# A transformer layer's attention keys: block-diagonal rows placed by DMA from DRAM images instead of by GpSimd products

## The reference

```python
x = _layernorm(x + _L0_attn_ref(x, Wq, bq, Wk, bk, Wv, bv))          # self-attention with interleaved rotary q, k
x = _layernorm(x + _L0_xattn_ref(x, ctx_1024, ctx_1024, mask, ...))  # 64 context rows, additive mask, dense after it
x = _layernorm(x + _L0_ffn_ref(x, W1, b1, W2, b2))                   # 128 -> 512 relu -> 128
# attention: scores = einsum('bhqd,bhkd->bhqk', q, k) / sqrt(8); softmax; einsum('bhqk,bhkd->bhqd', probs, v)
```

## Time and profile before

| | |
|---|---|
| median of 3 runs | 338.19 us (336.9 to 339.77) |
| profiled execution, span | 337.1 us |
| PE busy | 255.9 us (76%) |
| DVE busy | 225.2 us (67%) |
| ACT busy | 158.3 us (47%) |
| POOL busy | 151.3 us (45%) |
| DMA queue of SP | 20.86 MB, 22.7% of 16 engines |

### The profile page before, as it was taken

The page is one execution under the profiler, slowest core; times in us unless marked ns, Lnnn a source line. Parts: engine busy times, 40 slices in busy tenths (PEclk is TensorE's granted clock), DMA queues, the critical chain, the costliest instruction groups (busy, mean ns, idle before and its releaser), DMA issues.

```text
span 337.1 us, 5516 instructions
## 1 busy us (share of the span) xinstructions
PE 255.9 (76%) x1800; PEld 185.0 (55%) x1800; DVE 225.2 (67%) x471; ACT 158.3 (47%) x297; POOL 151.3 (45%) x159
## 2 busy tenths in 40 slices
PE   3146788779789889788978897888798786766752
PEld 1134355456566577566756665577476655544532
DVE  6534464867796877887788978877888464331322
ACT  1003347345666567455755764566357635305211
POOL 0027347539639733964296439633741321410010
PEclk9999989979999979997999999979799997957859
DMA  7232023115024211521152115111420120120000
GB/s 249 79 70 70 16 45 105 35 52 159 21 66 135 62 35 34 148 62 39 27 148 62 36 35 150 43 33 35 118 50 8 45 88 8 47 58 2 17 0 16
DMA packets 25413, 21.11 MB, mean 63 GB/s; under 512 B 6577, under 2 KB 22065, under 8 KB 25265
## 3 DMA queue, kind: packets, MB, share of 16 engines
q1 hardware_dynamic: 25392, 20.86, 22.7%
HBM read 8.79 MB, written 3.67 MB: 37 GB/s over the span
## 4 chain that ended last, share of the span: by engine, by line
PE 47%; DVE 34%; issue 9%; ACT 6%; DMA 1%; SPq 1%; POOL 0%; DVEq 0%; POOLq 0%; ACTq 0%
DVE neg_max L822 8%; PE scores_qk L389 7%; PE scores_kq L401 6%; DVE x L849 6%; PE pv_acc L422 5%; PE tail_ps L571 5%; PE tail_ps L606 4%; PE scores_qk L443 3%; DVE neg_maxx L894 3%; PE scores_qk L446 2%; DVE var_eps L844 2%; ACT probs L688 2%; PE scores_kq L465 1%; DVE max_parts L829 1%; DVE y L849 1%
## 5 line engine op out<-in xcount | busy, mean ns | idle before, releaser
L822 DVE TENSOR_REDUCE neg_max<-scores_qk 128x4 f32<-128x1024 f32 x64 | 78.1, 1221 | 33.5 <-PE scores_qk L389 32.8
L688 ACT ACTIVATE probs<-scores_kq 128x1024 f32<-128x1024 f32 x64 | 65.5, 1024 | 45.2 <-PE scores_kq L401 44.6
L293 POOL TENSOR_TENSOR k_diag<-slots,second_sb 128x1024 fp32r<-128x1024 f32 x31 | 58.7, 1892 | 29.8 <-DMA slots<-qk_parts 29.7
L389 PE MATMUL scores_qk<-k_diag,slots 96*128 96x512 f32 x128 | 47.5, 454 | 21.4 <-DVE neg_max L822 11.2
L401 PE MATMUL scores_kq<-slots,k_diag 128*128 128x256 f32 x256 | 49.8, 319 | 3.1 <-ACT probs L688 3.0
L401 PEld LDWEIGHTS scores_kq<-slots,k_diag 128*128 128x128 f32 x256 | 38.2, 205 | 11.2 <-issue 7.4
L1015 POOL TENSOR_TENSOR rstd<-var_eps,minus_half 128x2 f32<-128x2 f32 x24 | 16.8, 699 | 61.0 <-DVE var_eps L844 60.5
L422 PE MATMUL pv_acc<-probs,v_ones 128*32 128x256 f32 x512 | 36.7, 407 | 0.0
L389 PEld LDWEIGHTS scores_qk<-k_diag,slots 96*128 96x128 f32 x128 | 21.2, 206 | 26.6 <-issue 15.7
L1058 POOL TENSOR_TENSOR qx_parts<-qx,qx_parts 128x256 fp32r<-128x256 f32 x8 | 5.9, 733 | 46.7 <-DVE qx_parts L984 46.7
L849 DVE TENSOR_SCALAR x<-sum,mean_var,rstd 128x128 f32<-128x128 f32 x32 | 23.1, 764 | 0.8 <-POOL rstd L1015 0.8
(11 more groups left out here) (111 smaller groups left out, 489.1 us busy)
## 6 DMA issues: line engine op xcount, KB each, us to landing
slots<-qk_parts SPq DMA_DIRECT2D x96, 64.0 KB, 2.0
qx_slots<-qx_scratch SPq DMA_DIRECT2D x24, 128.0 KB, 2.7
qk_swapped<-qk SPq DMA_DIRECT2D x16, 128.0 KB, 2.3
qx_scratch<-qx_parts SPq DMA_DIRECT2D x8, 256.0 KB, 2.0
later_sb<-later SPq DMA_DIRECT2D x1, 1347.0 KB, 8.2
x_in<-x SPq DMA_DIRECT2D x8, 128.0 KB, 2.4
x_res<-x SPq DMA_DIRECT2D x8, 128.0 KB, 2.3
out<-y SPq DMA_DIRECT2D x8, 128.0 KB, 1.9
```

Of the source, the lines that this page charges most:

```text
L293: ops.tensor_tensor(k_diag[:, g, :, :].bitcast(F32R), slots[:, g, 1:2, :].to_broadcast([P, HQ, S]), row_head.to_broadcast([P, HQ, S]), ALU ...
L389: mm = pe.matmul(scores_qk[:, h * S:(h + 2) * S], sp_r[0:NROWS, g, 0, t * P:(t + 1) * P], kd_r[0:NROWS, g, h:h + 2, :], start=True, stop=True)
L688: nc.scalar.activation(probs[:, g % 2, 2 * half:2 * half + 2, :, :], scores_kq[:], ACT.Exp).then_inc(exp_done[g][half], 1)
L822: nc.vector.tensor_reduce(neg_max[:, g, t, :], scores_qk[:].rearrange("p (h k) -> p h k", k=S), AX.X, ALU.max, negate=True).then_inc(max_d ...
```

## The change

k's block-diagonal rows are no longer made by POOL. For self-attention, SP writes `qk_parts` to a DRAM image `z_self` in three DMAs (q high twice, k high twice, and both low parts), waits until they have landed, and loads from it `q_rows` (one DMA) and `k_diag` (four, one for each head position h, to every fourth partition). The zeros between are written once at the start: DVE clears `k_diag[:, 0]`, `kx_diag` and rows of `q_rows`, POOL clears `k_diag[:, 1]`. The columns for rows 96 to 103 are then copied once by ACT from `head_of_row`. `q_rows` and `k_diag` are double: element n uses part (n - 1) mod 2. To let one DMA reach the rows of a head, heads and dimensions are renumbered in the columns of the weights and biases: row p holds head 4 (p mod 4) + (p / 4 mod 4), and the rotary partner is 64 rows away, so that the swap goes by halves. Cross-attention gets images `z_kx` and `z_qx` in the same way. The hardware loop is written out, and counts are constants.

The core of the diff:

```diff
+        z_self = [nc.dram_tensor(f"z_self{b}", [8, P, S], F32, kind="Internal").ap() for b in range(2)]
+        z_qx = nc.dram_tensor("z_qx", [3, P, S], F32, kind="Internal").ap()
+        z_kx = nc.dram_tensor("z_kx", [3, P, SC], F32, kind="Internal").ap()
...
-        slots = sb("slots", [P, QUADS, 2, S])
-        k_diag = sb("k_diag", [P, QUADS, HQ, S])
+        q_rows = sb("q_rows", [P, 2, QUADS, S])
+        k_diag = sb("k_diag", [P, 2, HQ, QUADS, S])
...
-        def diagonal(eng, ops, g, loaded, used):
-
-            eng.wait_ge(slots_in[g], loaded)
-            if used:
-                eng.wait_ge(exp_ready[g][1], used)
-            ops.tensor_tensor(k_diag[:, g, :, :].bitcast(F32R), slots[:, g, 1:2, :].to_broadcast([P, HQ, S]),
-                              row_head.to_broadcast([P, HQ, S]), ALU.mult).then_inc(diag_done[g], 1)
...
+            def row_images(r):
+                z = z_self[r.n % 2].rearrange("(j s) p c -> p j s c", j=2)
+                if r.s > 1:
+                    sp.wait_ge(rows_in[(r.n - 1) % 2], 80 * ((r.n - 1) // 2))
+                sp.wait_ge(qk_hi_done, r.n)
+                for j in range(2):
+                    sp.dma_start(z[:, j, 0:2, :], qk_parts[:, 2 * j:2 * j + 1, :].to_broadcast([P, 2, S])
+                                 ).then_inc(z_hi_out, 16)
+                sp.wait_ge(qk_lo_done, r.n)
+                sp.dma_start(z[:, 0, 2:4, :], qk_parts[:, 1:4:2, :]).then_inc(z_lo_out, 16)
+
+            def row_loads(r):
+                b = (r.n - 1) % 2
+                z = z_self[r.n % 2]
+                q_image = z[0:3].rearrange("s (r g) c -> (s r) g c", g=QUADS)
+                k_image = z[3:6].rearrange("s (r h g) c -> (s r) h g c", h=HQ, g=QUADS)
+                sp.wait_ge(z_hi_out, 32 * r.n)
+                sp.wait_ge(z_lo_out, 16 * r.n)
+                if r.starts_prep:
+                    sp.wait_ge(diag_zeroed, 2)
+                if r.m:
+                    sp.wait_ge(exp_ready[3][1], r.m)
+                sp.dma_start(q_rows[0:NROWS, b, :, :], q_image).then_inc(rows_in[b], 16)
+                for h in range(HQ):
+                    sp.dma_start(k_diag[h:NROWS:HQ, b, h, :, :], k_image[:, h, :, :]).then_inc(rows_in[b], 16)
...
                 if r.prep:
-                    slot_loads(0, r.n, r.s)
-                    slot_loads(1, r.n, r.s)
+                    row_images(r)
+                    row_loads(r)
...
             def max_scores(g, t, done, free, free_count):
-
-                pe.wait_ge(diag_done[g], done)
+                b = (done - 1) % 2
+                pe.wait_ge(rows_in[b], 80 * ((done + 1) // 2))
+                if done == 1:
+                    pe.wait_ge(diag_ready, 3)
...
             act.wait_ge(first_in, 16)
-            iterations(act, "act", "w n n_32 s m t u", body)
+            act.wait_ge(diag_zeroed, 2)
+            for b in range(2):
+                for h in range(HQ):
+                    ins = nc.scalar.copy(k_diag[NROWS:NROWS + MROWS, b, h, :, :].bitcast(F32R), row_head(h, QUADS, S))
+                ins.then_inc(diag_ready, 1)
+            for h in range(HQ):
+                ins = nc.scalar.copy(kx_diag[NROWS:NROWS + MROWS, :, h, :].bitcast(F32R), row_head(h, QUADS, SC))
+            ins.then_inc(diag_ready, 1)
+            iterations(body)
...
-            nc.vector.memset(slots[NROWS:P, :, 0, :], 0.0)
-            nc.vector.memset(slots[NROWS:P, :, 1, :], 1.0)
+            nc.vector.memset(k_diag[:, 0, :, :, :], 0.0)
+            nc.vector.memset(kx_diag[:], 0.0)
+            nc.vector.memset(q_rows[NROWS:P, :, :, :], 0.0).then_inc(diag_zeroed, 1)
             nc.vector.memset(qx_slots[NROWS:P, :, :], 0.0)
-            nc.vector.memset(kx_slots[NROWS:P, :, :], 1.0)
...
+            nc.gpsimd.memset(k_diag[:, 1, :, :, :], 0.0).then_inc(diag_zeroed, 1)
```

More of the change, by code:

```diff
@@ L263, in rope_cosine, with iterations @@
+        def iterations(body):
+            for e in range(-2, B + 3):
+                body(Counts(e))
         def rope_cosine(eng, ops, r):
@@ L354, in body @@
+                    z = z_qx.rearrange("s p c -> p s c")
+                    sp.dma_start(z[:, 0:2, :], qx_parts[:, 0:1, :].to_broadcast([P, 2, S])).then_inc(qx_out, 16)
+                    sp.dma_start(z[:, 2, :], qx_parts[:, 1, :]).then_inc(qx_out, 16)
                 if r.mid:
[L355 removed]
+                    sp.wait_ge(kx_out, 32 * r.m)
                     if r.t:
                         sp.wait_ge(expx_ready[1], r.t)
[L358 to L360 removed]
+                    k_image = z_kx.rearrange("s (r h g) c -> (s r) h g c", h=HQ, g=QUADS)
@@ L693, in maxT @@
                 for t in range(QT):
-                    ins = nc.scalar.copy(slots[NROWS:NROWS + MROWS, g, 0, t * P:(t + 1) * P].bitcast(F32R),
+                    ins = nc.scalar.copy(q_rows[NROWS:NROWS + MROWS, (done - 1) % 2, g, t * P:(t + 1) * P].bitcast(F32R),
                                          prep_ps[t * P // QT:t * P // QT + MROWS, 0:P])
@@ L1090, in shape_constants @@
     sin = ((sign * np.sin(angle.astype(np.float64)))[:, None, :] * scale).reshape(P, 2 * S)
-    head = np.where(row < NROWS, (row % QROWS) // HD, np.where(row < NROWS + MROWS, row % HQ, -1))
+    head = np.where(row < NROWS + MROWS, row % HQ, -1)
     return {
@@ L1108 @@
     every_row = lambda v: np.broadcast_to(v[None, :], (P, v.shape[0]))
+    row = np.arange(P)
+    head_of = 4 * (row % 4) + row // 4 % 4
+    rotary = HD * head_of + 2 * (row // 16 % 4) + row // 64
+    plain = HD * head_of + row // 16
     maskT = a["mask_1x1xSxS2_fk1"][0, 0].T
```

179 lines of the change are left out of this document (56 added, 123 removed).

## The result

Four runs of the changed kernel have a median of 349.93 us (349.13 to 353.5), four of the kernel before on the same chip 338.5: a ratio of 1.037, 95% interval 1.030 to 1.044. It is slower by 11 us where 6.5 us less were forecast, and outside the range. The profiled span is 347.3 us against 337.1.

A forecast was written before the change was run, and what follows sets the result against it. TensorE sets the floor and waits for VectorE, which POOL's products hold up. Span 337.1 + 12.3 + 2.2 + 0.5 - 21.5 = 330.6; with 1.1 from span to median, 331.7 us; range 322 to 344.

The forecast's parts named there:

- The mechanism of the gain: VectorE instructions with SBUF operands stand still while POOL computes its products: 24.6 us of VectorE time, y's normalise more.
- the unrolled loop: Writing out the hardware loop, only three of eleven iterations: nothing, between -1 and +2 us.
- the three rivals: Stalls move house, rows land too late, or start costs little and the stalls all go (323.6 us, chance 0.15).
- The stalls move house: Rival: POOL's rope products start sooner and block VectorE instead; half the gains return, 342.4 us, chance 0.15.
- The rows land too late: Rival: the five row loads land after the first scores want them; 345.7 us at 2 us each, chance 0.12.
- Moved on SP's queue: SP's transfers reordered behind the images; kx_diag and qx_slots needed only in the next iteration: nothing.
- The two hops: DMA to a DRAM image and back, qk_low to first scores: 7.0 us, so +2.2 us at the start.
- slow end: Upper estimate of the two DMA hops, from later_sb's transfer rate: 8.3 us after qk_low.
- The cover: Steady iterations: 9.45 us from qk_low's end to the scores needing new rows, hides the hops and does not shrink.
- +0.5: Iteration 0: only 6.6 us from qk_low to the scores, rows up to 1.7 us late, taken as +0.5 us.
- The start's first term: Clearing and head-row casts before ScalarE's first xT copy, which starts at 18.2 in place of 5.86: +12.3 us.
- The gains: POOL's products removed: shorter VectorE stalls and TensorE waits, and no clock fall at L571, 21.5 us in sum.

The follow-up runs named there:

- the unread products: The changed kernel with POOL products of the old sizes put back, written to a buffer nobody reads or waits for: 368.08 us.
- the late casts: The changed kernel, with ScalarE copying the first element's xT and qk before it waits for the clearing and writes the twelve head-row casts: 335.6 us.

## Why the prediction was wrong

*The mechanism of the gain* held. VectorE's stall beside POOL's products is shown by the unread products. The gain is in the last three iterations before the drain (101.1 us before, 89.9 after), where L571 no longer takes 3.56 us. TensorE's waits for att1 before the drain fell by 6.5 us where 6.0 were counted, those at L600, 4.1 in all, are gone from the list, and the unrolled loop is worth nothing. None of the three rivals is what happened. "The stalls move house" is excluded by x's 339 ns and var_eps' 169 ns; what stayed is y's normalise at 528 ns, for example 1.59 us for a pair at 154.96 with POOL's qk_cos running from 155.19, and it had 746 before. "The rows land too late" happened in part, 6.5 us in five waits, 4.9 of them in iterations 1 and 2. For the largest part of the miss, the order on SP's queue, I had no rival.

*The step that failed* is "Moved on SP's queue": "kx_diag and qx_slots are needed only in the next iteration ... Nothing." By the program's counting that is true, but the next iteration begins a few us later: L416 at 160.11 uses what was issued at 156.19. I counted issues ("four and one in place of three and three") and gave them no length. With an issue time of 0.81 us for each kx load, the four put 3.2 us between the qx images and qx_slots. With these loads first the span is 8.2 us shorter. 5 us of it are waits, and the late casts give the same 5; the others come with a clock whose cause is open. I had looked at the steady iteration alone, where this is covered, and not at the drain, where qx_slots has no cover: there the kernel before already showed 1.16 us of waiting.

*The two hops* were mis-sized. "I take 7.0" between 5.9 and 8.3: measured 8.5 us from the end of qk_low to the scores at the start, beyond the slow end, and 9.3 in iteration 1 (qk_low ends at 80.9, L364 starts at 90.21). The issue term, 4 x 0.45 = 1.8, was 3.1; the image landed in 2.75 instead of 2.0. The strided loads' issue had no row in the trace of before, and I bounded it by the issue of transfers of another shape.

*The cover* was mis-sized the other way. "It does not shrink" was wrong: L571, now L544, lies between and went from 3.56 to 1.89 us by the very gain that I had counted. The kernel before could have told: one iteration on, with L571 at 1.89 us, the distance is 8.6 us (from 189.66 to 198.26), and 0.62 of these are TensorE's wait at L600 that I had counted as a gain too. After the change TensorE reaches the next scores after some 8 us, while the rows take up to 8.7, and it waits 0.2 to 1.2 us (from 170.33, the end of qk_low, to the scores at 178.95 with a wait of 0.61; from 200.49 to 209.23 with 0.72). In iteration 1 the kernel before had only 7.6 us (from 63.38 to 70.94), less than my slow end of 8.3; I had looked at iteration 0 and a steady one. There the rows took 9.3 us and TensorE waited 3.8. So "+0.5" for late rows was 6.5 us.

*The start's first term* was right: +12.3 forecast, +12.8 measured. Two small errors partly cancel in it: the clearing was over at 8.5 instead of 7.4, and the casts took 8.9 us instead of 9.5 (0.955 each for the wide ones, taken as 1.0). That it stands on the path is shown by the late casts, which bring the first scores 11.0 us forward.

*The gains,* 21.5 us: from the first scores to the end the changed kernel gained 6.3. Add the 6.5 of late rows and the 8.2 of SP's order, and it is 21.0. That this meets the forecast so closely is partly luck: the 8.2 hold the unexplained clock, and POOL's products cost 31 us in all when only they are taken out. By the spans, that is 27.7, the change must have paid some 38 us; the start's 16.5, the late rows and SP's order make 31, so about 7 us stay without a name.

In sum, 331.7 becomes, with 2.0 more at the start (0.5 up to the copy of xT, 1.5 in the hops), 6.0 more for late rows and 8.2 for SP's order, 347.9; 349.9 was measured.

## What carries over

When a queue's entries are exchanged for others, give each entry its issue time and follow the transfers behind it to the instruction that uses them, in the drain too, where nothing covers them; "next iteration" is no distance. A gain that is counted in one place shortens the cover in another: recompute the cover with the gains in it. One-time set-up that the first transfers do not need belongs behind them on its engine. And work that stalls a neighbour can go to an engine beside which the neighbour's instructions stay short, as ScalarE here, which beat the detour through DRAM; a detour's price is paid in every element and at the start, where nothing covers it.

## What was unexpected of the hardware

The issue time of a DMA on SP depends on its shape: 0.33 us for qx_slots (96 neighbouring partitions) where SP had waited for the images just before, 0.51 where it followed right behind kx's loads, 0.40 for most k loads to 24 neighbouring partitions, 0.78 for the same bytes to every fourth partition, 0.81 for kx's. Two memsets of 128x4096, one on POOL (3.51 us from 0.73) and one on VectorE (3.47 us from 1.66), ran side by side, at 0.87 us per 1024 columns on VectorE, as fast as VectorE's memset of 1024 columns behind them (0.91 us at 5.29, with POOL idle), where the products on POOL stop its two-column var_eps. The Trainium skill, "SBUF — State Buffer", section "Who interferes with whom", says as much: a VectorE instruction with at most one SBUF input outside the two-port modes does not contend; the rows agree. And the granted clock of the drain does not follow the length of TensorE's waits: 0.83 and 0.89 at the same waits of 2.8 and 3.9 us (2.6 and 3.8 in the changed kernel), 0.83 at waits of 0.3 and 1.2.
